# Cross-attention and routed FFN on one core: expert blocks write their rows plainly by page, and tokens gather and sum them beside the later blocks

## What is computed

```python
x = x + xattn(layernorm(x), ctx, ctx, Wq, Wk, Wv, Wo)        # 16 heads of 16
x = x + ffn(layernorm(x))
def ffn(xt):
    up_s   = einsum('th,seh->tse', xt, shared_up)             # 2 shared experts, width 128
    shared = einsum('tse,she->th', gelu(up_s), shared_down)
    probs  = softmax(xt @ router_w.T)                         # 16 routed experts
    topk_p, topk_i = top_k(probs, 4)
    up_r   = einsum('th,reh->tre', xt, routed_up)
    act    = gelu(up_r) * gate[:, :, None]                    # gate is zero outside the top 4
    return shared + einsum('tre,rhe->th', act, routed_down)
```

## Time and profile before

| | |
|---|---|
| median of 3 runs | 2591.99 us (2583.87 to 2592.43) |
| profiled execution, its span | 2592.7 us |
| busy: PE, DVE, ACT, POOL | 2097.7, 1587.4, 1257.4, 1216.0 us |
| moved by DMA | 538.93 MB, 208 GB/s over the span |
| attention | up to about 1480 us |
| blocks | about 1530 to 2318 us |
| sums | about 2330 us to the end |

### The profile page before, as it was taken

How to read it: one execution, slowest core, us unless ns; L and a number is a source line. 1 busy time by engine, 2 the same in 40 slices (tenths; PEclk the granted TensorE clock), 3 DMA queues, 4 the chain that set the end, 5 groups by cost and what they waited for, 6 DMA issues and landing times. The chain is left out here.

```text
span 2592.7 us, 55875 instructions
## 1 busy us (share of the span) xinstructions
PE 2097.7 (81%) x20646; PEld 1577.2 (61%) x20646; DVE 1587.4 (61%) x4387; ACT 1257.4 (48%) x2364; POOL 1216.0 (47%) x1648
## 2 busy tenths in 40 slices
PE   5888888988888888888888788999999889983310
PEld 3656565666656566666666567777777777762210
DVE  3566666666666666666665436666666666636556
ACT  3444445444544554444544336666666666650000
POOL 1034444443444444444444537777777777760000
PEclk8999999999999999999999699999999999996665
DMA  8244554545454545445453467777777777879999
GB/s 264 83 159 147 166 164 150 175 148 181 147 176 126 170 144 171 143 159 160 145 168 130 166 222 238 251 238 253 234 260 249 234 253 232 267 247 360 381 392 363
DMA packets 365486, 538.93 MB, mean 208 GB/s; under 512 B 100129, under 2 KB 297762, under 8 KB 361122
## 3 DMA queue, kind: packets, MB, share of 16 engines
q1 hardware_dynamic: 313186, 384.81, 46.6%
q0 software_dynamic: 52032, 150.54, 15.4%
HBM read 236.93 MB, written 298.32 MB: 206 GB/s over the span
## 5 line engine op out<-in xcount | busy, mean ns | idle before, releaser
L1076 POOL DMA_INDIRECT xs<-xn,idx x512 | 502.2, 981 | 605.4 <-DVE xn L922 149.5
L1101 POOL DMA_INDIRECT yt<-yo,ix x572 | 551.7, 965 | 188.9 <-issue 146.4
L686 ACT ACTIVATE pr<-A 128x512 f32<-128x512 f32 x512 | 264.4, 602 | 400.4 <-PE A L520 400.4
L817 DVE TENSOR_REDUCE ms<-A 128x4 f32<-128x512 f32 x512 | 316.8, 682 | 76.3 <-PE A L496 75.2
L600 PE MATMUL A<-ident,xr 128*128 128x128 f32 x1400 | 193.8, 283 | 79.0 <-DMA xr<-xs 61.4
L642 PE MATMUL A<-wt,hh 128*128 128x256 f32 x1144 | 249.4, 301 | 0.0
L600 PEld LDWEIGHTS A<-ident,xr 128*128 128x128 f32 x1400 | 163.3, 145 | 136.6 <-DMA xr<-xs 89.2
L642 PE MATMUL A<-wsh,act 128*128 128x256 f32 x512 | 130.4, 413 | 126.7 <-DVE rr L992 126.7
L956 DVE TENSOR_TENSOR xl<-A,xh 128x512 fp32r<-128x512 f32 x286 | 184.0, 683 | 76.0 <-ACT xh L737 75.0
L516 PE MATMUL A<-qt,km 32*128 32x128 f32 x4096 | 229.0, 343 | 0.6 <-DVE mt L837 0.6
L516 PEld LDWEIGHTS A<-qt,km 32*128 32x128 f32 x4096 | 190.6, 218 | 54.2 <-issue 49.1
(11 more groups left out here) (146 smaller groups left out, 4147.8 us busy)
## 6 DMA issues: line engine op xcount, KB each, us to landing
xr<-xs SPq DMA_DIRECT2D x143, 576.0 KB
xs<-empty SPq DMA_DIRECT2D x36, 2048.0 KB, 10.7
gb<-yt SPq DMA_DIRECT2D x32, 2048.0 KB, 15.4
xb<-in_x SPq DMA_DIRECT2D x32, 512.0 KB, 6.3
cg<-in_ctx_t SPq DMA_DIRECT2D x32, 512.0 KB, 4.0
yd<-xb SPq DMA_DIRECT2D x32, 512.0 KB, 3.5
x2d<-xn SPq DMA_DIRECT2D x32, 512.0 KB, 3.0
xr<-x2d SPq DMA_DIRECT2D x32, 512.0 KB
```

Of the source, the lines that this page charges most:

```text
L686: ac(pr[:, 4 * b:4 * b + 4, :].rearrange("p h s -> p (h s)"), banks[4 + b][:, :], ACT.Exp, scale=SCALE)\
L817: v.reduce_max(ms[n % 2][:, b, 0:4], banks[b][:, :].rearrange("p (h t) -> p h t", h=4), AX.X)\
L1076: q.indirect_dma_start(xs, bass.IndirectOffsetOnAxis(ap=idx[:, n, k:k + 1], axis=0), x2[g % 4][:, i, :], None).then_inc(sent[g % 4], 16)
L1101: q.indirect_dma_start(yt, bass.IndirectOffsetOnAxis(ap=ix[:, n % 8, k:k + 1], axis=0), yo[n % 4][:, k, :], None).then_inc(put[n % 4], 16)
```

## The change

Blocks no longer scatter. A block's 512 result rows are written by one plain DMA to `yl`, at the block's own page. The rows of `xs` carry the token's 256 numbers alone, `PAY` is gone, and with it the wait of SP. `R2` finds the four gates of every token (`gate`) beside the four places (`idx`), which both stay in SBUF. POOL then gathers: for each sequence, 128 tokens, four indirect DMAs read rows of `yl` by `idx` into one of six buffers `gb`, and DVE adds each to the token's `rr` with its gate, in four `scalar_tensor_tensor` of 128x256. POOL starts on group g when all pages up to `last_page(g)` are written.

```diff
+def last_page(g):
+    return min(NT - 1, (T * TOPK * (g + 1) + NRT * (RT - 1)) // RT - 1)
 def ffn_units():
     out = [("S", g) for g in range(AHEAD)]
     for t in range(NT):
         out.append(("R", t))
-        while g < G - LATE and (g - AHEAD + 1) * NT <= (t + 1) * (rest + 1):
+        if g < G and t >= last_page(g - AHEAD) + GT + LAG + 4:
             out.append(("S", g))
 def ffn_steps():
+            if UNITS[u + 2][0] == "S":
+                out.append(("YIN", UNITS[u + 2][1]))
         if 0 < u:
+            kind, t = UNITS[u - 1]
             out.append(("DN", u - 1))
+            if kind == "R" and t >= last_page(done // GT) + 1 + done % GT + LAG:
+                out.append(("SUM", done))
 # SP
+            def YIN(g):
+                wait(sp, stored[g % AHEAD], 16 * (g // AHEAD))
+                sp.dma_start(rr[g % AHEAD][:, :, :], token_rows(yd, g)).then_inc(rr_in[g % AHEAD], 16)
+            def DN(u):
+                if kind == "R":
+                    for b in FFN_BANKS["DN"](u):
+                        wait_drained(sp, b, "DN", u)
+                    sp.dma_start(block_rows(yl, n), yo[n % 3][:, :, :]).then_inc(put[n % 3], 16)
+            def SUM(n):
+                g, i = divmod(n, GT)
+                if i == GT - 1:
+                    sp.wait_ge(added, n + 1)
+                    sp.dma_start(token_rows(out, g), rr[g % AHEAD][:, :, :]).then_inc(stored[g % AHEAD], 16)
             def TR(u):
                     wait_filled(sp, 1, "TR", u)
-                    if kind == "R":
-                        sp.wait_ge(paid, 2 * (n + 1))
                     load_unit(u + 3)
 # ACT, DN of a block (DVE's half is gone)
-                    for q in range(2):
-                        ins = ac(yo[n % 4][:, q, :], banks[b][:, q * E:(q + 1) * E], ACT.Copy, scale=gt[:, n % 8, q:q + 1])
+                    wait(act_e, put[n % 3], 16 * (n // 3))
+                    for k, b in enumerate(FFN_BANKS["DN"](u)):
+                        wait_filled(act_e, b, "DN", u)
+                        ac(yo[n % 3][:, 2 * k:2 * k + 2, :].rearrange("p q e -> p (q e)"), banks[b][:, :], ACT.Copy)\
+                            .then_inc(drain[b], 1)
 # DVE, R2 (the scan and two copies into the payload are gone)
+                many = [P, GT, TOPK, NRT]
+                link(v.tensor_tensor(same[:, :, :, :], key[:, :, :].unsqueeze(2).broadcast_to(many),
+                                     pk[:, :, 0:TOPK].unsqueeze(3).broadcast_to(many), ALU.is_equal))
+                link(v.tensor_tensor(same[:, :, :, :], same[:, :, :, :],
+                                     prob[g % 2][:, :, 0:NRT].unsqueeze(2).broadcast_to(many), ALU.mult))
+                v.reduce_sum(gate[:, g * GT:(g + 1) * GT, :].rearrange("p i k -> p (i k)"),
+                             same[:, :, :, :].rearrange("p i k r -> p (i k) r"), AX.X)
# DVE
+            def SUM(n):
+                for b in FFN_BANKS["DN"](GROUP[g]):
+                    wait_drained(dve, b, "DN", GROUP[g])
+                dve.wait_ge(gb_in[n % NGB], 16 * TOPK * (n // NGB + 1))
+                y = rr[g % AHEAD][:, i, :]
+                for k in range(TOPK):
+                    wait(dve, add_done, (TOPK - 1) * n + k)
+                    v.scalar_tensor_tensor(y, gb[n % NGB][:, k, :], gate[:, n, k:k + 1], y, ALU.mult, ALU.add)\
+                        .then_inc(add_done if k < TOPK - 1 else added, 1)
 # POOL
+            for n in range(B):
+                if i == 0:
+                    for k in range(3):
+                        pool.wait_ge(put[k], 16 * len(range(k, last_page(g) + 1, 3)))
+                wait(pool, added, n - NGB + 1)
+                for k in range(TOPK):
+                    q.indirect_dma_start(gb[n % NGB][:, k, :], None, yl[0:(last_page(g) + 1) * RT, :],
+                                         bass.IndirectOffsetOnAxis(ap=idx[:, n, k:k + 1], axis=0)).then_inc(gb_in[n % NGB], 16)
```

More of the change, by code:

```diff
@@ L79, in ffn_units @@
         out.append(("R", t))
-        while g < G - LATE and (g - AHEAD + 1) * NT <= (t + 1) * (rest + 1):
+        if g < G and t >= last_page(g - AHEAD) + GT + LAG + 4:
             out.append(("S", g))
             g += 1
-    return out + [("S", n) for n in range(G - LATE, G)]
+    return out + [("S", n) for n in range(g, G)]
 UNITS = ffn_units()
-ORDER = sorted(range(G), key=lambda g: ((g + 1) / (G - LATE) if g < G - LATE else (g - G + LATE + 1.5) / (LATE + 1), g))
 UPS = [(u, k) for u, (kind, _) in enumerate(UNITS) for k in range(1 if kind == "R" else NSH)]
 BLOCK = {n: u for u, (kind, n) in enumerate(UNITS) if kind == "R"}
+GROUP = {n: u for u, (kind, n) in enumerate(UNITS) if kind == "S"}
 def ffn_steps():
@@ L101, in ffn_steps @@
         if u + 2 < NU:
-            kind, n = UNITS[u + 2]
             out.append(("TR", u + 2))
-            if kind == "R":
-                out.append(("PAY", n))
+            if UNITS[u + 2][0] == "S":
+                out.append(("YIN", UNITS[u + 2][1]))
         if 0 < u:
+            kind, t = UNITS[u - 1]
             out.append(("DN", u - 1))
[L108 to L114, removed]
+            if kind == "R" and t >= last_page(done // GT) + 1 + done % GT + LAG:
+                out.append(("SUM", done))
+                done += 1
         if u + 2 < NU and UNITS[u + 2][0] == "R":
             out.append(("WC", UNITS[u + 2][1]))
-    return out + [("SUM", f) for f in range(done, G)]
+    return out + [("SUM", n) for n in range(done, B)]
 ATT = attention_steps()
@@ L157, in program @@
         idx = sb("idx", [P, B, TOPK], I32)
+        gate = sb("gate", [P, B, TOPK])
         flat = sb("flat", [1, 2 * P], I32)
         wsh = sb("wsh", [P, NSH, 2, E])
-        x2 = [sb(f"xn2_{k}", [P, GT, W]) for k in range(4)]
-        t32 = sb("t32", [P, KC, T])
         wr = sb("wr", [P, KC, NRT])
@@ L173, in program @@
         pk = sb("pk", [P, GT, 8])
-        ones = sb("ones", [P, GT * NRT], BF16)
-        place0 = sb("place0", [P, G])
-        place = sb("place", [P, GT * NRT])
+        same = sb("same", [P, GT, TOPK, NRT])
         base, bound, shift = (sb(k, [P, NRT]) for k in ("base", "bound", "shift"))
@@ L194, in sa @@
             return early.enter_context(nc.sbuf_tensor(name, shape, dt))
+        x2 = [sa(f"xn2_{k}", [P, GT, E]) for k in range(4)]
+        t32 = sa("t32", [P, KC, T])
+        empty = sa("empty", [P, 2, E])
         wqs, wks, wvs, wos = (sa(k, [P, KC, E]) for k in ("wqs", "wks", "wvs", "wos"))
@@ L226, in sc @@
             return late.enter_context(nc.sbuf_tensor(name, shape, dt))
+        gb = [sc(f"gb{k}", [P, TOPK, E]) for k in range(NGB)]
+        rr = [sc(f"rr{k}", [P, GT, E]) for k in range(AHEAD)]
         wt = [sc(f"wt{k}", [P, 2, 2, E], F32R) for k in range(3)]
@@ L263, in program @@
         blank_set, emptied = sem("blank_set"), [sem(f"emptied{k}") for k in range(4)]
-        wc, x_hi, paid = sem("wc"), sem("x_hi"), sem("paid")
+        wc, x_hi = sem("wc"), sem("x_hi")
         gelu, h_hi = sem("gelu"), sem("h_hi")
[L266 to L269, removed]
+        put = [sem(f"put{k}") for k in range(3)]
+        gb_in, rr_in = [sem(f"gb_in{k}") for k in range(NGB)], [sem(f"rr_in{k}") for k in range(AHEAD)]
+        add_done, added, stored = sem("add_done"), sem("added"), [sem(f"stored{k}") for k in range(AHEAD)]
         block = es.enter_context(nc.Block())
@@ L432, in _ @@
+            run(FFN, {"TR": TR, "YIN": YIN, "DN": DN, "SUM": SUM})
+            for k in range(AHEAD):
+                sp.wait_ge(stored[k], 16 * len(range(k, G, AHEAD)))
         @block.tensor
@@ L859, in RL @@
                     .then_inc(drain[1], 1)
-            def payload(g):
-                return x2[g % 4][:, :, E:W].rearrange("p i (r c) -> p i r c", c=2)
             def R1(g):
@@ L915, in R2 @@
                 link(v.scalar_tensor_tensor(key[:, :, :], key[:, :, :], 1.0, gm[g % 2][:, 0:GT, :], ALU.add, ALU.mult))
-                v.tensor_tensor_scan(place[:, :], ones[:, :], gm[g % 2][:, 0:GT, :].rearrange("p i r -> p (i r)"),
-                                     place0[:, g:g + 1], ALU.mult, ALU.add)
                 for i in range(GT):
@@ L921, in R2 @@
                 link(ins)
-                v.tensor_copy(payload(g)[:, :, :, 1], place[:, :].rearrange("p (i r) -> p i r", i=GT)).then_inc(rows_set, 1)
+                many = [P, GT, TOPK, NRT]
[5 more added lines that the diff above has]
+                             same[:, :, :, :].rearrange("p i k r -> p (i k) r"), AX.X)
                 link(v.tensor_scalar(idx[:, g * GT:(g + 1) * GT, :], pk[:, :, 0:TOPK], -1.0, None, ALU.add))
@@ L971, in DN @@
                 kind, n = UNITS[u]
-                own = FFN_BANKS["DN"](u)
-                if kind == "R":
-                    wait_filled(dve, own[1], "DN", u)
-                    dve.wait_ge(paid, 2 * (n + 1))
-                    wait(dve, put[n % 4], 16 * GT * (n // 4))
-                    for q in range(2, 4):
```

(15 more changed lines are left out.)

134 lines of the change are left out of this document (32 added, 102 removed).

## The result

The changed kernel takes 2342.78 us (2338.93 to 2347.87, four runs), the kernel before 2590.39 in the runs beside it: a ratio of 0.905 (0.9031 to 0.9069). The forecast was 2398 with a range from 2345, so the kernel came out 55 us faster than forecast and just under the range. The profiled execution spans 2336.8 us.

The account below looks back on a forecast made before the run. POOL was taken to bound the old blocks at 5.25 us each, with a last stretch waiting for DMA. The terms 1535 + 82 + 50 + 612 + 74 + 40 + 5 gave 2398 us, range 2345 to 2490.

Parts of the forecast that it names:

- the tail: Behind the last block: its store, 16 gathers, a sum and one more block's way through the stages, 40 us.
- attention: Stretch before the blocks: R2 gives DVE 0.6 us more a group, less DMA gains little; bounds -5 and +19, taken +5 us.
- the start of the blocks: Before block 1: YIN loads yd rows ahead, 5 us given back for attention's scatters; block 1 at 1535 us.
- Blocks 1 to 20: Blocks before any sum: ACT's wider evictions make a block 4.1 us with a little waiting, 82 us in all.
- Blocks 21 to 28: Blocks each with a sum: POOL's pace of 5.3 us each, plus 7.8 for shared group 6, 50 us.
- The rounds: 25 rounds of one shared group and four blocks: PE's 22.8 us plus 1.7 added, 24.5 each, 612 us.
- The coupling itself: In the rounds: 1.7 us added to each for DVE's late blocks and SP waiting for an out store.
- rival (e): Sums wait for gathers, DVE stalls PE at each group, overlap partly lost: 2440 to 2550 us; 0.18 together with (a).
- (a): DMA binds the rounds at 26.1 to 29 us each: 2475 us; chance 0.18 together with (e).
- (b): DVE holds POOL off, each add blocking a gather for its whole 0.45 us, 1.72 a gather: 2507 us; chance 0.07.
- (c): Coupling is free: PE alone decides the rounds, blocks without shared groups run at DVE's 4.7 us: 2343 us; chance 0.09.
- (d): Slower than before: a gather costs POOL more than a scatter; at 2.0 us each, 2646 us; chance 0.05.

Follow-up runs that it names:

- the first run: The changed kernel with the old blank payload writes put back as work alone, to a DRAM tensor that nobody reads: 2357.0 us, ratio 0.9103.
- the reordered kernel before: The kernel before, with SP filling the next set of xs behind the load of x instead of in front, same DMAs: 2562.2 us, ratio 0.990.
- the run with more bytes: The changed kernel with 128 KB more to load for each block into a spare tile on SP's queue, 18.7 MB in all: 2349.9 us, ratio 0.9083.

## Why the prediction was wrong, step by step

**Right in direction, nature and most terms.** POOL paced the old blocks, if not alone, and passed it on through SP. PE is the bound behind the change but for 1 us a round, and the old tail is gone. The gated add is 0.486 us (0.49 taken), a sequence's sum 2.05, a round of PE 22.6 (22.8), and the tail 47.5 behind the last gelu, where 40 was taken from a few us later.

**The step that failed: attention.** It said "Rows of 1024 instead of 1152 bytes and no payload blanks take DMA work from a stretch where the DMA share is 0.48: nothing gained, or a few us", and took +5. What came is 22.4 us gained: attention's last scatter, before and then after:

```profile
1510.71 0.96 POOL L1076 DMA_INDIRECT xs<-xn,idx  x1 [0.30 <-issue]
```

```profile
1488.28 0.96 POOL L1009 DMA_INDIRECT xs<-xn,idx  x1 [0.30 <-issue]
```

That is the whole error of 27 us before block 1, of the 61 between sum and span: the start of the blocks gave 5.3 us, where 5 was taken. By the first run the blanks are 14 to 18 of it. The mean share of 0.48 hid that these DMAs come in one burst in front of a load that DVE needs. The prediction looked at SP's queue for the blocks and not for attention. R2 has 0.73 us more of DVE's work a group (0.6 was taken), and it cost 0.3 us a group at most, by 43.0 us with it and 42.7 without it in the reordered kernel before.

**Terms that were sized too high.** Blocks 1 to 20 at 4.1 us took 3.78, and PE is what filled them, 77.92 of 78 us (1512 to 1590):

```profile
1512.00:1590.00 78.00, 77.92 (x536) 68.75 (x536) 52.84 (x82) 73.23 (x121) 1.42 (x2) 1.00 0.75 265
```

The prediction put the wider evictions, 0.23 us, on top of ACT's free block of 3.75 as if ACT were full. It wasn't: between the rows it stood for 0.50 us:

```profile
2291.08 1.06 ACT L729 ACTIVATE wt<-wall 128x1024 fp32r x1 [0.50 <-issue]
```

Blocks 21 to 28 took 43.1 us instead of 50. POOL's sequence was 5.0 us and not 5.3, because a gather is 0.946 us at the median and 0.969 in the mean; that is 2.4 us. The rest is an overlap that the sum denied: it set shared group 6 behind POOL's eight sequences, and POOL gathers on while PE works on the group, in the changed kernel without a gap from 1588.28 to 1628.51. At the end POOL's smaller time gives the 5 us. The rounds had 1.7 us added for coupling where 1.0 was real, 17 us over all.

**The coupling itself** was placed on DVE's late blocks and SP's wait for `stored`. No row shows a wait for `stored`. It was what rival (e) names, in small: DVE waiting for a group's gathers, 87.0 us in 52 waits over 24 rounds, or 3.6 us a round, of which 1.0 reached PE. One block of distance takes it away whole.

**The rivals.** (a) and (b) fell by the run with more bytes and by POOL's rows. (c) named 2343 us, by luck: it had the rounds at PE's pace, and they weren't; what brought the kernel there is mostly the attention, which (c) left as it was. (d) would have needed 1.9 us for a gather.

## What to carry to other kernels

A mean DMA share says nothing about a queue in which a load that is needed soon stands behind a fill with thousands of short runs; look at how long each issue of the queue takes, and put the load first. In a pipeline that is fixed by hand, a consumer placed where its producer is just done on average stalls the whole order each time it isn't: give it one more step, as long as a buffer is free, before making either side faster. And when a bound is removed, the new floor was readable: PE's free blocks and back-to-back groups in the old trace gave the round to 1%.

## What the runs showed of the hardware

- The issue of a DMA on SP grew with what had been issued just in front of it: 5.96 and 7.52 us for a load of 512 KB behind 2.25 MB of fill, 3.28 behind 2 MB in runs of 1 KB, 1.16 behind the same in runs of 2 KB, 0.51 with nothing in front.
- A DMA share of 0.96 was not saturation: in the stretch from 1660 to 2200 the rate rose from 331 to 353 GB/s, 12 MB more, and the 18.7 MB more in the whole run cost 7 us.
- A gather by 128 indices costs POOL what a scatter does, 0.95 and 0.30 us of issue. Beside DVE's gated adds of 0.485 us it depends on where it starts. Of 512 gathers 84 took over 0.96 us, and 83 of these started 0.09 to 0.35 us into an add; each was longer by what was left of that add, less 0.13 us. Those that started earlier or later in an add took 0.95 us, as with no add at all; the add lasted up to 0.544 us when a gather started in its first 0.09 us. POOL in the changed kernel, with DVE's four adds from 2268.74 on, 0.52 us from start to start, and from 2273.23 on:

```profile
2268.18 0.95 POOL L1023 DMA_INDIRECT gb<-yl,idx  x1 [0.30 <-issue]
2269.43 1.13 POOL L1023 DMA_INDIRECT gb<-yl,idx  x1 [0.30 <-issue]
2270.87 0.95 POOL L1023 DMA_INDIRECT gb<-yl,idx  x1 [0.30 <-issue]
...
2273.37 1.15 POOL L1023 DMA_INDIRECT gb<-yl,idx  x1 [0.30 <-issue]
```

  The gather at 2269.43 starts 0.17 us into the second add. The Trainium skill's page "SBUF — State Buffer", section "SBUF: two separate sides", has the operation that starts first keep the shared port for its whole instruction, and the rows agree: a held gather waits for the end of the add under way. What rival (b) made of it, a whole add for every gather, they don't show: a gather is held once, by 0.27 us at most and 0.02 us in the mean.
